# A vision-tower layer on one core: gate weights spread by PE from bf16 pieces, expert parts in another order, mixing phase rearranged

## The reference, cut to what matters

```python
q = x @ Wq + bq;  k = x @ Wk + bk;  v = x @ Wv + bv
y = einsum(dg * (q @ k^T), v) @ Wo + bo              # mixing of tokens
h = where(y >= 0, y, prelu_a * y)
n = layernorm(h)                                      # state-space part
A = exp(-softplus(n @ Wd + bd)); u = (1 - A) * (n @ Wb + bb) * (n @ Wx + bx)
s_t = A_t * s_(t-1) + u_t                             # scan over the tokens
h = h + ((n @ Wc + bc) * s) @ Wy + by
n = layernorm(h)                                      # experts: 16, each 64 -> 128 -> 64
w = top-2 of softmax(n @ gate_w + gate_b), renormed to a sum of 1
h = h + sum_e w_e * ((silu(n @ w1_e) * (n @ w2_e)) @ w3_e)
```

## Time and profile before

| | us |
|---|---|
| median of 3 runs | 327.31 |
| lowest and highest | 323.82, 329.04 |
| span of the profiled execution | 331.5 |

### The profile page before, as it was taken

The page is one execution under the profiler, slowest core; times in us unless marked ns, Lnnn a source line. Parts: engine busy times, 40 slices in busy tenths (PEclk is TensorE's granted clock), DMA queues, the critical chain, the costliest instruction groups (busy, mean ns, idle before and its releaser), DMA issues.

```text
span 331.5 us, 4678 instructions
## 1 busy us (share of the span) xinstructions
PE 257.1 (78%) x1645; PEld 156.7 (47%) x1645; DVE 160.1 (48%) x283; ACT 119.7 (36%) x283; POOL 98.2 (30%) x119
## 2 busy tenths in 40 slices
PE   8999999988935976258829995169964899952995
PEld 7443332532411323136529884168642698621563
DVE  1453649789805993167705610053410466710664
ACT  1302561764108711467534541022320344311341
POOL 4000000004760077303771047600476000674000
PEclk9999999999985999658965997555796599995699
DMA  7999800000111101332221675995121323021101
GB/s 191 371 388 278 170 0 0 4 0 12 40 51 57 33 20 52 89 95 73 55 58 44 154 160 131 209 222 114 41 59 28 83 65 78 19 44 20 34 16 32
DMA packets 45990, 29.74 MB, mean 90 GB/s; under 512 B 32688, under 2 KB 41072, under 8 KB 45456
## 3 DMA queue, kind: packets, MB, share of 16 engines
q1 hardware_dynamic: 30416, 23.15, 27.1%
q10 hardware_dynamic: 12480, 3.15, 4.3%
q0 software_dynamic: 3072, 3.15, 3.9%
HBM read 20.46 MB, written 8.98 MB: 89 GB/s over the span
## 4 chain that ended last, share of the span: by engine, by line
PE 52%; another core or an unknown queue 19%; ACT 11%; DVE 10%; issue 7%; ACTq 0%; POOL 0%; DVEq 0%; POOLq 0%
PE ring L1013 10%; PE ring L971 9%; PE turn L988 7%; PE side L1025 5%; PE acc L816 4%; PE ring L802 4%; ACT squares L611 3%; PE side L843 3%; DVE mixed L1141 2%; PE ring L759 2%; PE side L775 2%; ACT n L629 2%; PE acc L934 1%; DVE state L1190 1%
## 5 line engine op out<-in xcount | busy, mean ns | idle before, releaser
L559 POOL DMA_INDIRECT slots<-n,slot_i x48 | 47.8, 996 | 121.9 <-DVE slot_i L1256 108.2
L1283 DVE TENSOR_TENSOR act<-ring,silu 128x512 f32<-128x512 f32 x56 | 38.4, 690 | 89.5 <-ACT silu L681 68.6
L569 POOL DMA_INDIRECT back_v<-results,slot_i x48 | 46.5, 968 | 81.4 <-DMA results<-res 67.7
L681 ACT ACTIVATE silu<-ring 128x512 f32<-128x512 f32 x56 | 33.3, 597 | 78.7 <-remote 38.5
L1141 DVE TENSOR_TENSOR mixed<-ring,dg 128x1024 f32<-128x1024 f32 x32 | 38.6, 1218 | 19.5 <-remote 10.9
L816 PE MATMUL acc<-mixed,v 128*64 128x512 f32 x128 | 34.3, 628 | 8.6 <-DVE mixed L1141 8.4
L802 PE MATMUL ring<-kq 64*128 64x512 f32 x128 | 33.5, 629 | 0.0
L1013 PE MATMUL ring<-nT,w_sb 64*128 64x256 f32 x128 | 24.2, 459 | 8.8 <-issue 8.0
L971 PE MATMUL ring<-slots_t,w_shared 64*128 64x128 f32 x192 | 19.8, 328 | 13.7 <-issue 12.7
L988 PE MATMUL turn<-w_sb,act 128*128 128x64 f32 (+1 forms) x192 | 29.1, 314 | 0.0
L988 PEld LDWEIGHTS turn<-w_sb,act 128*128 128x128 f32 x192 | 27.3, 226 | 3.0 <-issue 2.2
(11 more groups left out here) (150 smaller groups left out, 306.5 us busy)
## 6 DMA issues: line engine op xcount, KB each, us to landing
dg<-dgT SPq DMA_DIRECT2D x8, 512.0 KB, 7.8
dg<-given SPq DMA_DIRECT2D x8, 512.0 KB, 15.7
slots<-zeros SPq DMA_DIRECT2D x3, 1024.0 KB, 13.2
w_shared<-w SPq DMA_DIRECT2D x48, 64.0 KB, 2.2
slots<-slots SPq DMA_DIRECT2D x12, 256.0 KB
results<-res ACTq DMA_DIRECT2D x12, 256.0 KB, 2.9
w_sb<-w SPq DMA_DIRECT2D x2, 1024.0 KB, 14.3
xs<-xT SPq DMA_DIRECT2D x4, 256.0 KB, 6.5
```

Of the source, the lines that this page charges most:

```text
L559: pool.indirect_dma_start(out=slots_dram[r], out_offset=bass.IndirectOffsetOnAxis(ap=slot_i[:, r, k, i:i + 1], axis=0), in_=n2[:, u % 2, i ...
L569: pool.indirect_dma_start(out=back_v[:, r, i, k, :], out_offset=None, in_=results_dram[r], in_offset=bass.IndirectOffsetOnAxis(ap=slot_i[: ...
L681: s.activation(silu[:, n % 2], hidden_banks(n)[:, :, 0:PAIRS * P], ACT.Silu).then_inc(silu_done, 1)
L1283: dve.tensor_tensor(act[:, n % ACT_BUFS], hidden_banks(n)[:, :, PAIRS * P:2 * PAIRS * P], silu[:, n % 2], ALU.mult).then_inc(act_done, 1)
```

## The change

- The gate weights no longer go through DRAM. DVE splits the weights (`dispatches`) into three bf16 parts whose sum is exact (`high`, `mid`, `low`, 3 of every 3 adjacent columns), PE turns them in 4 bf16 matmuls, ACT copies them once, and for each of the 16 experts one bf16 matmul with a 0/1 matrix `pick` puts the sum of the three parts on the 64 partitions of each batch (`spread_gate`). `weigh` reads that PSUM bank. POOL builds `pick` in the unused `xs` with a few instructions. The ten DMAs on SP are gone.
- `DENSE_RUNS` becomes (0, 0, 0, 32): part 2 stands directly behind part 1, all dense items at the end.
- The first two turnings of loaded rows go to the scores' banks instead of `acc`, so they stand before the last two `pv` steps, and the first pieces of the experts start at beat 62 instead of 65. SP loads the first two pairs of rows before the first weights of part 1, not behind them.
- `center2` and the logits product become one product with 160 columns (`cg`). `scale_rows` comes behind the squares and the deviation of the next unit. `place`, `slots`, `spread`, `owner_row`, `owners` move one beat later, so that the state-space step of DVE stands before them.
- At the start: 30 warm-up matmuls instead of 50 and then 20, the first projection ahead of the product of Wv and Wo, the second half of v and the projections K1 and Q1 at beat 2, and the loads of `vec` and `wvo` on ACT's queue instead of SP's.

The diff, cut:

```diff
-    "center2": (16, 17), "turn_h": (21, 17), "count": (24, 21), "owner_row": (27, 14), "prelu": (0, 0),
+    "center2": (16, 17), "turn_h": (21, 19), "count": (24, 21), "owner_row": (28, 14), "prelu": (0, 0),
...
-    "logits": (19, 18), "mark0": (19, 19), "one0": (22, 19), "mark1": (22, 20), "one1": (22, 21), "place": (25, 24),
+    "logits": (19, 18), "mark0": (19, 19), "one0": (22, 19), "mark1": (22, 20), "one1": (22, 21), "place": (26, 24),
...
-WEIGHTS_AFTER = (-2, -2, -2, -2, -1, 3, 3, 6, 7, 7, 9, 11)
+WEIGHTS_AFTER = (-2, -2, -2, -2, 1, 3, 3, 6, 7, 7, 8, 8)
...
-FFN_BEAT = 65
-FFN_RATES = (1, 2, 1, 2, 1, 1, 0, 1, 0, 1, 1, 1, 2, 0, 1, 1, 1, 1, 2, 4, 0, 3, 0, 1)
+FFN_BEAT = 62
+FFN_RATES = (4, 4, 0, 1, 1, 0, 2, 1, 1, 0, 2, 0, 1, 0, 1, 0, 0, 0, 1, 2, 1, 2, 4, 0, 3, 0, 1)
...
-DENSE_RUNS = (0, 0, 8, 24)
+DENSE_RUNS = (0, 0, 0, 32)
...
-WARM = 50
-WARM2 = 20
+WARM = 30
...
-            def spread_given(i):
...
-                    sp.dma_start(weighed[rows_b(b), e, :],
-                                 given_dram[b, e, :].unsqueeze(0).broadcast_to([D, NE // GIVEN_LOADS, CW])).then_inc(ld_given[i], 16)
...
             def center2(u):
                 pe.wait_ge(hT2_done, u + 1)
                 for t in range(TT):
-                    mm = pe.matmul(side[:, 1, t * P:(t + 1) * P], hT[:, u % 2, t * P:(t + 1) * P], center_m[:, :],
+                    mm = pe.matmul(side[:, t // 2, t % 2 * CG:(t % 2 + 1) * CG], hT[:, u % 2, t * P:(t + 1) * P], cg[:, :],
                                    start=True, stop=True)
                 mm.then_inc(cen_done[1], 1)
-                for t in range(TT):
-                    mm = pe.matmul(side[:, 0, t * 2 * NE:(t + 1) * 2 * NE], hT[:, u % 2, t * P:(t + 1) * P], gate_w[:, :],
...
             def turn_slots(i):
                 if i == 0:
+                    pe.wait_ge(mixed_done, ALL_STEPS - 1)
+                if i == 2:
                     pe.wait_ge(relu_done, 2 * UNITS)
                 pe.wait_ge(ld_slots[i % SLOT_BUFS], 16 * (i // SLOT_BUFS + 1))
-                if i >= 1:
+                if i >= 3:
                     pe.wait_ge(sin_done, i)
...
+            def spread_gate(e):
+                pe.wait_ge(given_done, 1)
+                pe.wait_ge(nT2_done, 1)
+                if e >= 2:
+                    pe.wait_ge(weighed_done, e - 1)
+                if e == NE // 2:
+                    pe.wait_ge(sin_done, ROUTED // 2)
+                pe.matmul(spread_bank(e), pick[:, e, :], given_t[:, :], start=True, stop=True).then_inc(spread_out, 1)
...
             def weigh(e):
 
-                dve.wait_ge(ld_given[e // (NE // GIVEN_LOADS)], 16 * BH)
+                dve.wait_ge(spread_out, e + 1)
+                dve.wait_ge(mixed_done, ALL_STEPS)
                 dve.wait_ge(nT2_done, 1)
-                dve.tensor_tensor(weighed[:, e, :], weighed[:, e, :], nT2[:, :], ALU.mult).then_inc(weighed_done, 1)
+                dve.tensor_tensor(weighed[:, e, :], spread_bank(e), nT2[:, :], ALU.mult).then_inc(weighed_done, 1)
```

More of the change, by code:

```diff
@@ L372, in build_layer, with spread_bank, cg_tiles @@
         x_bank = side[:, 0, :]
-        def given_bank(b):
-            return side[0:NE, 1 - b, :]
+        given_bank = side[:, 1, :]
+        def spread_bank(e):
+            if e % 2 == 1:
+                return side[:, 1, :]
+            return side[:, 0, :] if e < NE // 2 else acc[:, :]
         def turned_sum(c):
             return side[:, 1, 0:GB * D]
+        def cg_tiles():
+            return side[:, :, 0:2 * CG].rearrange("p k (t c) -> p k t c", c=CG)
         def count_bank(u):
@@ L736, in _ @@
                     norm_std(0, u)
+                for u in due("rows2", m):
+                    if u < LAST:
+                        scale_rows(u)
                 for u in due("tanh_table", m):
```

143 lines of the change are left out of this document (79 added, 64 removed).

## The result

| | before | changed |
|---|---|---|
| median, us | 327.2 (4 runs) | 354.5 (4 runs) |
| lowest and highest | 323.8, 329.0 | 350.7, 357.1 |
| span of the profiled execution | 331.5 | 348.9 |

A forecast was written before the change was run, and what follows sets the result against it. PE's work plus six bursts of POOL's indirect DMAs bound the kernel. Terms of -2.6, +1.0, -8.0, +3.0, -3.5, +3.2, 0 and -1.0 sum to -7.9 us, off the median 327.3: 319.4, range 304 to 333.

The forecast's parts named there:

- First rows early: Before unit 3's h is turned, early expert pieces fill PE's holes: -8.0 us, bounds 0 and -8.7.
- Start: At the kernel's start, fewer warm-up matmuls take work off PE: -2.6 us, bounds -1.3 and -3.5.
- Table loads: On ACT, four more table changes at 1.283 us, partly covered by holes: +3.0 us, bounds 0 and 5.1 + 0.6.
- Mixing phase: End of the second hole: merged product and reordering gain nothing kept, later `place` delays bursts: +1.0 us, bounds -4 to +5.
- Gate weights: First gather's hole: removing eight broadcast loads gives -3.5 us; 16 spread matmuls on PE, less saved transposes, cost +3.2.
- Part 2 behind part 1: Order of routed and dense work: PE's work stays the same, 0 us, bounds -5 to +5.
- Clock: Less idle time at 130 to 148 leaves PE less at the lower clock: -1 us, bounds 0 and -5.
- the chain of unit 3: Rival: from 139.5 to the turning of h, early pieces delay PE's in-order chain; slower, 341 us, chance 0.15.
- h later than 176: Sign that the forecast is wrong: the turning of unit 3's h comes later than 176 us.
- The rival with the transfers as the cause of the hole: At 200 to 217, data traffic starves PE, so all 12.7 us of idle time go; 310 us, chance 0.18.
- the rule of the Trainium skill on fetching instructions: Possible way for transfers to make the hole: sequencers fetch instructions through DMA queues; no row showed a late fetch.

The follow-up runs named there:

- set 1: Runs on one chip with the holes, kernel before at 327.5 us: one part of the change alone, or one part undone.
- set 4: Runs on a chip with hardly any holes, kernel before at 260.0 us: the changed kernel again (274.9 us) and edits of ACT's order.
- set 2: Runs on a chip with the holes, kernel before at 328.4 us: place of the spreads, old beats, gathers left out or made plain copies.
- late_experts: Changed kernel with its experts begun at beat 65 at the rates of before, all else changed: 345.2 us, ratio 1.052 to before.
- late_old_beats: Changed kernel with experts from beat 65 and the mixing phase's beats and row scalings of before: 337.8 us, ratio 1.032 to before.
- spread_only: Kernel before with only its gate weights spread by PE from three bf16 pieces, in one bank: 333.2 us, ratio 1.016.
- 3 to 5: Three later sets of runs on chips with the holes nearly gone; kernel before at 259.0, 260.0 and 258.3 us.

## Why the prediction was wrong

The sum was -7.9 us; on the chip it was +27. The step that failed is *First rows early*, forecast at -8.0 and measured at +9. Term by term:

- *Start, -2.6.* Right: -3.5 measured. The first projection stands at 4.2, as named.
- *First rows early, FFN from beat 62, -8.0.* It failed in sign: the worst that its bounds allowed was 0. I priced the PE work that would fill holes and never listed what the same pieces put into ACT's queue. The first `take_slots` waits 7.5 us there, with `keep` of unit 2 behind it, and the first silus stand ahead of the deviations of units 2 and 3 and of h of unit 2. Undoing the early pieces gave 9 us back in set 1. What they do was taken apart only in set 4, on a chip nearly without holes: of some 16 us of loss there, `keep` ahead of `take_slots`, an edit of ACT's queue alone, gave back 7.9, and moving the hidden layers with their silus 6.2. On a chip with the holes the waits of 7.5 and 4.0 us stand in the profile, but these two edits did not run.
- *Table loads, +3.0.* Right that they are four, 5.1 us, and that nT and product d are queued behind them; but they came with their silus, which wait for PE and are waited for: with them and their hidden layers moved back, 6.2 us go.
- *Mixing phase, +1.0.* Too small: 6 to 7 us in set 2, beyond the far bound of +5. The second and third group of scatters begin 5 us later with the new beats (119.0 and 156.8 in late_experts, 113.8 and 151.9 in late_old_beats); which edit of the phase does it is open. The merged product and the order of SP's loads were not run alone.
- *Gate weights, -3.5 + 3.2.* The loads gave 2 us of the first gather's hole; the spreads cost 7.2 us of work in place of 4.1. In spread_only, which adds 4.6 us of PE's idle time by its single bank, it is +5 in all; in the changed kernel it was not measured alone. I had scaled the duration of 512 columns from matmuls of 128 columns that ran back to back; a spread stands alone and takes 0.39, not 0.26. And I counted `weigh` as free on an idle DVE, where in a slow stretch the gated product stands behind it.
- *Part 2 behind part 1, 0.* Right: +0.4%.
- *Clock, -1.* Wrong sign: the mean granted clock fell from 0.846 to 0.833 between the two profiled executions, and the timed ones of before in set 1 have 0.853 to 0.864. The prediction read 0.57 to 0.77 in five of six stretches; the earlier trace rows have it in all six.

Added up, start -3.5, early pieces +9, mixing phase +6 to 7, gate weights +5 and order of parts +1.4 make 18 to 19 of the 27 us, an estimate, since the parts were measured in different kernels and need not add. Some 8 us no experiment removed; 5.8 us of more idle time in the last gather point to the place, not to the cause.

Of the rivals, the chain of unit 3 came nearest, with 341 and a chance of 0.15; its sign, h later than 176, was the one that showed. But its price was of PE's pieces in front of the chain, and its 341 is near 354 partly by luck. Of the 14 us given back in set 4, 7.9 came through ACT's queue, which it does not have. The rival with the transfers as the cause of the hole is out: PE's idle time in that stretch, 11.7 of 23.7 us, is as in the other groups without any broadcast.

One cause of the holes that I had weighed, the rule of the Trainium skill on fetching instructions ("Runtime: NRT & Kernel Launch", section "Instruction fetch mechanics"), finds no support in the stretch looked at. In before, between 165 and 180, where PE is idle for 5.8 us, the queues are these:

```profile
q10 hardware_dynamic: 1040, 0.26, 7.7%
q0 software_dynamic: 320, 0.33, 6.1%
q1 hardware_dynamic: 608, 0.15, 4.6%
```

No packet of an instruction queue is among them, and in the whole span there are 22. What makes all engines start late beside a group of indirect transfers, and why it shows in sets 1 and 2 and not in 3 to 5, stays open.

## What to carry to other kernels

When work is moved forward, write down what it puts into the queue of every engine, and for each waiting instruction what stands behind it: here a copy of 0.6 us held `keep` for 7.5 us. Undo such an edit engine by engine, not only as a whole; one number (`keep` one beat earlier) gave half of the loss back on the chip where it ran. And take the ratio on more than one chip and occasion before idle time in a profile is treated as the kernel's own.

## What the runs showed of the hardware that I had not expected

- The kernel before took 327 to 328 us on three occasions and 258 to 260 on three later ones, on other chips. The pace of the indirect DMAs is the same (0.94 us and 0.30 between two), but in the first 20.0 us of the changed kernel's first group of gathers PE is busy for 10.2 us on the one kind and for 19.2 on the other.
- On a chip with the holes, 48 plain transfers of the same size in place of 48 indirect ones took 44 of 328 us off (the rows copied are then not those looked up). A plain one takes 0.53 us of POOL (8.4 for 16).
- In such a stretch a DVE instruction started 9.1 us after DVE was free, with what it waits for done before that (`weigh` at 286.15 above).
- A bf16 matmul of 128x512 takes 0.39 us at full clock and 0.61 at the lower level.
